# Attention with a fused output projection on one core: units ordered by group of heads, output sums loaded and stored per set

## The reference

```python
xn = _layernorm(x)
qkv = xn @ w_qkv                        # 1024 -> 4096 (q) + 1024 (k) + 1024 (v)
scores = einsum('bqhgd,bkhd->bhgqk', q, k) * 128 ** -0.5
bias = -slopes * sqrt(i - j)            # for j <= i, else -inf (causal)
attn = softmax(scores + bias)
out = einsum('bhgqk,bkhd->bqhgd', attn, v).reshape(B, S, 4096)
attention = out @ w_o                   # 4096 -> 1024
# beside it: ffn = xn @ W.T + b + a low-rank term of the rank that a softmax gate picks
return x + attention + ffn
```

## Time and profile before

| | us |
|---|---|
| median of 3 runs | 2558.14 (2558.04 to 2559.82) |
| the profiled execution's own time | 2558.13 |
| its span, first to last instruction | 2556.3 |
| TensorE busy in the span | 2429.0 (95%) |
| VectorE | 1593.5 (62%) |
| ScalarE | 1442.5 (56%) |
| GpSimd | 884.0 (35%) |

### The profile page before, as it was taken

One profiled execution on the slowest core, in us unless ns is written; L12 is line 12 of the kernel. 1 busy time (PEld: TensorE's weight loads), 2 busy tenths in 40 slices (PEclk: granted clock), 3 DMA queues, 4 the chain that ended last, 5 costly groups with the idle time before them and its releaser, 6 DMA issues.

```text
span 2556.3 us, 35119 instructions
## 1 busy us (share of the span) xinstructions
PE 2429.0 (95%) x12128; PEld 2042.3 (80%) x12128; DVE 1593.5 (62%) x2905; ACT 1442.5 (56%) x3131; POOL 884.0 (35%) x1158
## 2 busy tenths in 40 slices
PE   6999999997999999998899999999999999999998
PEld 4787888885778888887788888888888888888886
DVE  6657445565756445654666777667766776667765
ACT  4432133334533133333877777777777777777774
POOL 3211000001231000000464556545654556445654
PEclk8999999998999999999999999999999999999999
DMA  4546354464355435445613231332334231332221
GB/s 148 183 132 222 116 191 159 176 219 176 103 159 202 153 137 198 169 176 189 227 67 116 102 121 68 115 116 100 110 146 182 100 116 67 124 115 101 80 108 69
DMA packets 94704, 355.25 MB, mean 139 GB/s; under 512 B 8874, under 2 KB 9018, under 8 KB 85569
## 3 DMA queue, kind: packets, MB, share of 16 engines
q1 hardware_dynamic: 62480, 233.43, 25.5%
q0 software_dynamic: 32048, 119.60, 13.5%
HBM read 235.02 MB, written 117.97 MB: 138 GB/s over the span
## 4 chain that ended last, share of the span: by engine, by line
PE 79%; DVE 10%; issue 5%; ACT 4%; DMA 1%; POOL 1%; ACTq 0%; DVEq 0%; SPq 0%; POOLq 0%
PE ps L648 25%; PE ps L650 25%; PE ps L649 25%; PE ps L835 4%; DVE wo L1130 3%; DVE acc L1398 1%; ACT probs L1049 1%; DVE probs L1367 1%; DVE pt_lo L1130 1%; ACT wo L895 1%; ACT res_hi L895 1%; DVE stats L1144 1%; ACT rows L924 1%; DVE w_lo L1130 1%; DMA qk_s<-res_hi 0%
## 5 line engine op out<-in xcount | busy, mean ns | idle before, releaser
L895 ACT ACTIVATE w_hi<-raw 128x1024 fp32r<-128x1024 f32 x196 | 207.0, 1059 | 559.3 <-PE ps L650 440.8
L1130 DVE TENSOR_TENSOR w_lo<-raw,w_hi 128x1024 fp32r<-128x1024 f32 x196 | 239.1, 1224 | 358.2 <-ACT w_hi L895 358.1
L1398 DVE TENSOR_TENSOR acc<-ps,acc 128x512 f32<-128x512 f32 x448 | 296.7, 684 | 226.7 <-issue 195.4
L648 PE MATMUL ps<-x_hi,w_hi 128*128 128x512 f32 x1120 | 436.3, 390 | 0.0
L650 PE MATMUL ps<-x_hi,w_lo 128*128 128x512 f32 x1120 | 435.8, 389 | 0.0
L649 PE MATMUL ps<-x_lo,w_hi 128*128 128x512 f32 x1120 | 435.7, 389 | 0.0
L648 PE MATMUL ps<-wo,op_hi 128*128 128x512 f32 x896 | 367.0, 410 | 50.4 <-issue 30.6
L1035 ACT ACTIVATE probs<-probs,neg_max 128x512 f32<-128x512 f32 (+3 forms) x512 | 283.6, 565 | 200.8 <-DVE neg_max L1367 200.8
L650 PE MATMUL ps<-wo,op_lo 128*128 128x512 f32 x896 | 354.8, 396 | 0.0
L649 PE MATMUL ps<-wo,op_hi 128*128 128x512 f32 x896 | 353.1, 394 | 0.0
L1367 DVE CUSTOM_DVE_ANT_0 probs<-ps,bias 128x512 f32<-128x512 f32 (+3 forms) x512 | 220.3, 484 | 95.3 <-PE ps L650 93.3
(11 more groups left out here) (156 smaller groups left out, 4983.9 us busy)
## 6 DMA issues: line engine op xcount, KB each, us to landing
raw<-w_all SPq DMA_DIRECT2D x70, 1024.0 KB, 5.5
q<-qk_s SPq DMA_DIRECT2D x128, 512.0 KB, 3.3
qk_s<-res_hi POOLq DMA_DIRECT2D x40, 1024.0 KB, 4.6
wo_raw<-w_o SPq DMA_DIRECT2D x64, 512.0 KB, 5.5
qk_s<-res_a POOLq DMA_DIRECT2D x20, 1024.0 KB, 9.1
qk_s<-res_b POOLq DMA_DIRECT2D x20, 1024.0 KB, 5.3
k<-qk_s SPq DMA_DIRECT2D x32, 512.0 KB, 5.7
v<-v_s SPq DMA_DIRECT2D x32, 512.0 KB, 8.5
```

What stands on the lines that cost most here:

```text
L648: pe.matmul(to, st_hi, mv_hi, start=start, stop=False, skip_group_check=True)
L895: nc.scalar.activation(to, source, ACT.Copy).then_inc(signal, 1)
L1130: nc.vector.tensor_tensor(to, source, high.bitcast(F32), ALU.subtract).then_inc(signal, 1)
L1398: nc.vector.tensor_tensor(to, fill[f % 2][:, :], to, ALU.add).then_inc(s_acc, 1)
```

## The change

1. `unit(n)`: the group is outermost, then the pair, the batch and the head. A group's weights are now made once for four sets: 8 makings (`GROUPS`), every 16 units. The bias of the next group is made in the last of the four sets.
2. `acc`: for each set the four tiles of its batch are loaded from `acc_s` (`take_in`) and stored back (`put_out`), to `out` in the last group. Both are issued by SyncE in halves of two tiles.
3. `fills(n)`: the output products of a set start one unit later, (n-2) instead of (n-1), and all loops are one unit longer.
4. `shaped(n)`: the operands of a set are made in a unit ahead of their products; GpSimd does 3, 1, 3 and 1 block sums in the four units and ScalarE its high halves in one place, behind the exponentials.
5. The making: block sums of weights in units F-3 (step 4), F-2 (steps 2, 3) and F-1 (step 5), where F is the unit of first use. High halves: steps 0 and 1 at the end of F-2, 3 and 2 at the end of F-1, 4 and 5 ahead of the exponentials of F, 6 at its end. Low halves: steps 0 and 1 between the sums of F-1, 3 at its end, 2 ahead of the inverses of F, 4 between its sums, 5 and 6 at its end.

```diff
--- before.py
+++ after.py
@@ -55,12 +55,21 @@
...
-OUT_SUMS = ((0, 3), (1, 3), (0, 2), (0, 6), (0, 4), (1, 2), (1, 6), (1, 4))
-OUT_SPLITS = ((), (0, 1), (2, 3, 4), (5, 6))
-WO_SUMS_IN = ((4,), (2,), (3, 5), ())
-GROUPS = SETS // 2
+OUT_SUMS = ((0, 3), (0, 2), (0, 6), (0, 4), (1, 3), (1, 2), (1, 6), (1, 4))
+SUM_SHARES = (range(0, 3), range(3, 4), range(4, 7), range(7, 8))
+GROUPS = KV_HEADS
+GROUP_UNITS = SETS // GROUPS * G
+WO_SUMS = (4, 2, 3, 5)
+WO_SUMS_IN = {7: (4,), 8: (2, 3), 9: (5,)}
+WO_ORDER = (0, 1, 3, 2, 4, 5, 6)
+HIGHS_FIRST = {10: (4, 5)}
+HIGHS_LAST = {8: (0, 1), 9: (3, 2), 10: (6,)}
+LOWS_EARLY = {10: (2,)}
+LOWS_MIDDLE = {9: (0, 1), 10: (4,)}
+LOWS_LAST = {9: (3,), 10: (5, 6)}
@@ -289,27 +298,21 @@
         def unit(n):
-            pr, rest_ = n // (2 * HEADS), n % (2 * HEADS)
-            g, b, h = rest_ // (2 * G), rest_ // G % 2, rest_ % G
-            return pr, g, b, h
+            return n // (2 * G) % PAIRS, n // GROUP_UNITS, n // G % 2, n % G
...
-            s, c = (n - 1) // G - 1, (n - 1) % G
+            s, c = (n - 2) // G - 1, (n - 2) % G
...
-            s, c = n // G - 1, n % G
-            if c == 0:
-                return ([], [(s, 0)]) if 0 <= s < SETS else ([], [])
+            s, c = (n - 1) // G - 1, (n - 1) % G
             if not 0 <= s < SETS:
-                return [], []
-            return {1: ([(s, 1), (s, 2), (s, 3)], [(s, 4), (s, 5), (s, 6)]),
-                    2: ([], [(s, i) for i in range(7, 11)]),
-                    3: ([], [(s, i) for i in range(11, 14)])}[c]
+                return s, [], []
+            return s, [OUT_SUMS[i] for i in SUM_SHARES[c]], list(SHARES[c])
@@ -325,29 +328,21 @@
-        def making(n):
-            group, since = (n - 2) // (2 * G), (n - 2) % (2 * G)
-            return (group, since) if n >= 2 and group < GROUPS and since < G else (None, None)
-        def out_splits(n):
-            group, since = making(n)
-            return [] if group is None else [(group, i) for i in OUT_SPLITS[since]]
-        def out_sums_in(n):
-            group, since = making(n)
-            return [] if group is None else [(group, i) for i in WO_SUMS_IN[since]]
-        WO_SUMS = (4, 2, 3, 5)
+        def making(n, table):
+            group, place_ = (n + G) // GROUP_UNITS, (n + G) % GROUP_UNITS
+            return [(group, i) for i in table.get(place_, ())] if group < GROUPS else []
...
+        def made(group, step):
+            return STEPS * group + WO_ORDER.index(step) + 1
...
-            return PARTS * (2 * group - 1) + STEPS + step + 1
+            return PARTS * (SETS // GROUPS * group - 1) + STEPS + step + 1
@@ -412,7 +407,7 @@
...
                 half, pair = i // 2, i % 2
-                head = group % KV_HEADS * G + 2 * pair
+                head = group * G + 2 * pair
@@ -423,37 +418,46 @@
...
                         out_block(0, i)
-                if n in range(3, 7):
-                    sp.wait_ge(s_store_h, stores_h(2, VALUES, 0))
-                    sp.wait_ge(s_store_a, stores_r(2, VALUES, 0))
-                    sp.wait_ge(s_store_b, stores_r(2, VALUES, 0))
-                    for tt in ((0, 2), (1, 3), (4, 6), (5, 7))[n - 3]:
-                        sp.dma_start(acc[:, tt, :], acc_s[bass.ds(tt * P, P), :]).then_inc(s_acc_in[tt], 16)
-                group = n // (2 * G)
-                if n % (2 * G) == G + 3 and group + 1 < GROUPS:
+                group = n // GROUP_UNITS
+                if n % GROUP_UNITS == 2 * G + 2 and group + 1 < GROUPS:
...
-            def store_out(pr, b, t):
-                tt = b * QT + t
-                sp.dma_start(out[bass.ds((pr * TT + tt) * P, P), :], acc[:, tt, :]).then_inc(s_out[tt], 16)
-            def results(n):
-                for b in range(2):
-                    last = SETS // PAIRS - 2 + b
-                    if n == G * (last + 2) + 3:
-                        for t in range(QT):
-                            sp.wait_ge(s_acc, PARTS * last + (STEPS if t % 2 == 0 else PARTS))
-                            store_out(0, b, t)
-                    if n == G * (last + 2) + 4:
-                        for t in range(QT):
-                            tt = b * QT + t
-                            sp.wait_ge(s_out[tt], 16)
-                            sp.dma_start(acc[:, tt, :], acc_s[bass.ds((TT + tt) * P, P), :]).then_inc(s_acc_in[tt], 16)
+            def sums_home(pr, b, t):
+                return bass.ds((pr * TT + b * QT + t) * P, P)
+            def take_in(s, tile):
+                pr, _, b, _ = unit(s * G)
+                for t in (tile, tile + 2):
+                    if s >= 2:
+                        sp.wait_ge(s_out[b * QT + t], 16 * (s // 2))
+                    sp.dma_start(acc[:, b * QT + t, :], acc_s[sums_home(pr, b, t), :]).then_inc(s_acc_in[b * QT + t], 16)
+            def put_out(s, tile):
+                pr, g, b, _ = unit(s * G)
+                sp.wait_ge(s_acc, PARTS * s + STEPS * (tile + 1))
+                for t in (tile, tile + 2):
+                    to = out if g == GROUPS - 1 else acc_s
+                    sp.dma_start(to[sums_home(pr, b, t), :], acc[:, b * QT + t, :]).then_inc(s_out[b * QT + t], 16)
+            def sums_in_and_out(n):
+                if n == 3:
+                    sp.wait_ge(s_store_h, stores_h(2, VALUES, 0))
+                    sp.wait_ge(s_store_a, stores_r(2, VALUES, 0))
+                    sp.wait_ge(s_store_b, stores_r(2, VALUES, 0))
+                if n in range(3, 7):
+                    take_in((n - 3) // 2, (n - 3) % 2)
+                for s in range(SETS):
+                    since = n - G * s - 10
+                    if since in (0, 2):
+                        put_out(s, since // 2)
+                    if since in (1, 3) and s + 2 < SETS:
+                        take_in(s + 2, since // 2)
@@ -475,13 +479,11 @@
...
                 out_weights(n)
-                results(n)
-            for t in range(2 * QT):
-                sp.wait_ge(s_acc, PARTS * (SETS - 2 + t // QT) + (STEPS if t % 2 == 0 else PARTS))
-                store_out(PAIRS - 1, t // QT, t % QT)
+                sums_in_and_out(n)
+            for n in range(UNITS, UNITS + 3 * G):
+                sums_in_and_out(n)
             for tt in range(TT):
-                sp.wait_ge(s_out[tt], 16 * PAIRS)
+                sp.wait_ge(s_out[tt], 16 * SETS // 2)
@@ -610,35 +612,21 @@
...
                 if step == 5:
-                    pool.wait_ge(s_wo_lo, STEPS * group + 2)
+                    pool.wait_ge(s_wo_lo, made(group, 1))
...
-            for n in range(UNITS + G + 1):
-                at_once, later = shaped(n)
-                s, c = n // G - 1, n % G
-                for group, step in out_sums_in(n) if c == 0 else ():
-                    wo_sums(group, step)
-                if c == 0 and at_once + later:
-                    pool.wait_ge(s_at_raw, G * s + 2)
-                    for tile, k in OUT_SUMS[0:2]:
-                        out_sum(s, tile, k)
-                if at_once:
+            for n in range(UNITS + G + 2):
+                s, new_sums, new = shaped(n)
+                if new_sums:
                     pool.wait_ge(s_at_raw, G * (s + 1))
-                    for tile, k in OUT_SUMS[2:4]:
-                        out_sum(s, tile, k)
-                for part in at_once:
-                    out_low(*part)
-                if at_once:
-                    out_sum(s, *OUT_SUMS[4])
-                if c == 2 and later:
-                    for tile, k in OUT_SUMS[5:8]:
-                        out_sum(s, tile, k)
-                for part in later:
-                    out_low(*part)
-                for group, step in out_sums_in(n) if c != 0 else ():
+                for tile, k in new_sums:
+                    out_sum(s, tile, k)
+                for part in new:
+                    out_low(s, part)
+                for group, step in making(n, WO_SUMS_IN):
@@ -852,8 +840,8 @@
...
                 f = PARTS * s + part
-                if s % 2 == 0 and tile == 0:
-                    pe.wait_ge(s_wo_lo, STEPS * (s // 2) + k + 1)
+                if s % (SETS // GROUPS) == 0 and tile == 0:
+                    pe.wait_ge(s_wo_lo, made(s // (SETS // GROUPS), k))
@@ -1055,7 +1043,7 @@
...
                 if k in (0, 1, 5):
-                    act.wait_ge(s_at_raw, G * s + (2 if k == 0 else G))
+                    act.wait_ge(s_at_raw, G * (s + 1))
@@ -1097,12 +1085,12 @@
...
                 leave(number(pr, MATRICES - 1, STEPS - 1))
-            for n in range(UNITS + G + 1):
-                at_once, later = shaped(n)
+            for n in range(UNITS + G + 2):
+                s, _, new = shaped(n)
...
                     outputs(n - 2)
-                for part in at_once:
-                    out_high(*part)
+                for part in making(n, HIGHS_FIRST):
+                    out_split(*part)
@@ -1110,11 +1098,11 @@
...
                         exponential(n, c)
-                for part in later:
```

(27 more changed lines are left out.)

## The result

Five runs of the changed kernel have a median of 2546.35 us (2544.82 to 2546.99), five of the kernel before, beside them, 2559.82 us (2558.04 to 2561.91). The ratio is **0.9946, with an interval of 0.9932 to 0.9961**: 13.5 us faster by the medians where 54.4 were forecast, and outside the forecast range of 2484 to 2521. The span of the profiled execution went from 2556.3 to 2545.1 us, -11.2.

A forecast was written before the change was run, and what follows sets the result against it. TensorE's gaps were taken to bound the kernel: making stalls of 72.3 us falling to 20.3 (-52.0), the end -1.9 and -0.5, the start 0, sum -54.4. Span 2556.3 becomes 2501.9, plus 1.8 gives 2503.7 us; range 2484 to 2521.

The forecast's parts named there:

- What bounds the kernel: Stage from about 1215 us: TensorE sets the pace, only its gaps can be won; each making costs 4.88 us.
- Groups first: Weights made once per group for all four batches: 8 makings for 16, stalls in the stream from 15 to 7.
- The wait for the copied output goes: In F, products two units after a set's last output give its copy a whole unit's cover, ending that wait.
- The new making, walked through: Engine orders followed through F-1, F and F+1: 2.9 us lost per making, ends 0.3 and 4.9; 7 make 20.3 us.
- each restart of TensorE: Within a making: 0.2 us for each of three restarts of a stopped TensorE, 0.6 us of the 2.9.
- GpSimd and VectorE: Mutual blocking at low halves: longer by at most 0.57 us; at 1.78 us each in F, a making costs about 4.6.
- Sums loaded and stored: Four 512 KB tiles out and in per set, some 190 GB/s for 110; costed at nothing, covered by early issue.
- Rival 3: Slower: sums come late at every set's first addition; 3 us of wait each gives 2594 us; chance 0.04.
- The end: Last set: wait for operands covered, -1.9 us; two stores instead of three behind the last sum, -0.5 us.
- The start: First units and first making: one more unit without products against fewer low halves; taken as 0, ends -3.3 and +4.9 us.
- Rival 2: A making costs as now or more, by low halves or two high halves in F: 2517.7 us, 2539 at 8; chance 0.25.
- what would show it: Signs to check: 158.6 us over 16 units, 1.2 to 1.8 us wait before F's attention product, DMA near 190 GB/s.

The follow-up runs named there:

- group_only: Kernel before with only the group order and the loads and stores of sums; products, operands and weights stay where they were: 2521.21 us, ratio 0.9848.
- high5_last: Changed kernel with the high half of step 5 moved from ahead of the exponential of F to the end of F: 2515.17 us, ratio 0.9824.
- no_sum5: Changed kernel with GpSimd's fourth weight sum cut from 1024 columns to 8, so step 5's operand is not the reference's: 2521.36 us, ratio 0.9852.
- sum5_sooner: spread, with GpSimd's fourth weight sum made between the operands' lows and F's first add ahead of low half 2: 2494.26 us, ratio 0.9746.
- kept_busy: Changed kernel with 50 unread identity transposes on TensorE ahead of the third product of every F: 2531.17 us, ratio 0.9888.
- lows_apart: Changed kernel with low halves 0 and 1 moved within F-1, behind the maxima and ahead of the inverses: 2542.18 us, ratio 0.9937.
- no_traffic: Changed kernel without most stores and loads of the sums and the waits on them, so most output sums are missing: 2544.55 us, ratio 0.9942.
- all_moves: low6_next, with the first group's weights also made one by one from unit 1 on: 2486.23 us, ratio 0.9714.
- low6_next: sum5_sooner with low half 6 moved from the end of F to behind the maxima of F+1: 2493.46 us, ratio 0.974.
- spread: Changed kernel with the weights' high and low halves placed by what waits for them, low half 2 ahead of F's first sum: 2509.99 us, ratio 0.9806.

## Why the prediction missed

The sign held, the number did not. By its own steps:

- **What bounds the kernel: right.** TensorE's gaps, 4.88 us per making before, none elsewhere. Where no making is, the stage runs at 100 of 100 us.
- **Groups first: right.** Seven stalls for fifteen, 56 high halves of weights. group_only has this part alone: 38.8 us, where 72.3 - 7 x 5.3 = 35 of stalls is what its own makings give. They cost 5.3 (5.4 over all seven) and not 4.8 each, with a gap of 2.8 us in F for 2.0 and a fall of the clock behind each of the seven.
- **The wait for the copied output goes: right.** No wait of that kind is left. F-1 lost 1.25 us and now loses nothing, F+1 1.01 and now 0.02.
- **The new making, walked through: this step failed.** It forecast 2.9 us per making, and 8.2 were lost. It asked when VectorE is free for the maxima, a sum and the attention product, and never when **low half 2 is due**. TensorE's third product of F needs it 1424.8 - 1413.1 = 11.7 after T of F-1. By the walk's own times it stands behind the last low copy at 14.8 and takes 1.35: 16.15, so a gap of 4.5 us was in the numbers of the text, unseen. The other 1.5 are the times themselves: the fourth sum ended at 12.5 for 11.3 (the two lengthened lows, 3.41 for 1.45, and the sum, 3.79 for 2.83), the low copies at 16.5 for 14.8, the low half took 1.14. 16.46 + 1.14 + 0.04 = 17.64, and 17.64 - 11.68 = 5.96, the gap. high5_last and no_sum5 show that this chain is the cause, sum5_sooner that without its two waits a making costs 1.6 us, within the 0.3 to 4.9 of the text.
- **A term that was missing: the clock.** The walk took 0.2 us for each restart of TensorE. Behind this gap it runs at 1.2 GHz for 4.7 us, 2.0 us per making and 13.8 us in all (kept_busy). The kernel before had the price too: a fall behind four of its fifteen gaps in F, some 1.1 us each, so it could be read there, and the average of 4.82 holds some of it. The making of the earlier trace rows, from which the walk took its times, is one without a fall.
- **GpSimd and VectorE: undersized.** The text took at most 0.57 us per low half, on VectorE alone. The Trainium skill (SBUF — State Buffer, "Who interferes with whom") calls the shared ports an exclusive lock, so either side can lose; the traces agree: a low part of GpSimd goes from 0.73 to 1.7, four pieces of a sum from 2.8 to 3.8, and a low half of VectorE from 1.21 to 1.84. In lows_apart one low half stayed at 1.21 beside sums of GpSimd that were lengthened. What this adds to the gap stays open, since lows_apart moved it and did not remove it; 4.5 of the 5.96 us come out of the walk's own times without it.
- **Sums loaded and stored: right.** 191 GB/s for the "some 190" forecast, loads land in 5.1 us, no engine waits for one, and no_traffic, without most of them, is 1.8 us faster, no more. Rival 3 did not come.
- **The end: right**, 3.3 us better for its work by the timeline against 2.4 forecast, and the 1.67 us behind the last attention product are gone.
- **The start: wrong**, 0 forecast and 6.0 us lost for its work, just outside the text's ends. Its making has the same chain: TensorE waits 2.49 us at 1252.00 for a low copy and 3.65 at 1266.35 for a low half, and runs slow behind both (0.77 and 0.80). The fall behind the first gap is not certain: in kept_busy, whose code is the same up to there, the gap is 2.50, the matmul behind it takes 0.47 and the unit 9.4 us for 12.2, so 2.8 of the 6.0 us are this fall. all_moves spread those halves over the first seven units and takes 68.5 us from the first T to the ninth for the 71.4 of low6_next.

Of the 43.2 us between forecast and span, 52.0 - 15.7 = 36.3 are the makings, 6.0 the start, 1.8 the stage before (code left alone), and -0.9 the end. **Rival 2** was the case that came, by its strong form of 8 us a making (2539), which the range had left out. Its reason was half right: it named the two high halves ahead of the exponential, but priced them by the weakest number, "as now".

The section on what would show it named 158.6 us from T to T over 16 units; 164.11 lie between two gaps. It named 1.2 to 1.8 us ahead of the attention product as the wait in F; the wait stood one output product earlier.

## What to carry to other kernels

When steps are re-ordered by hand, list for each result that the bound engine reads when it is due and when it is made, every one of them; the one that was left off the list was the one that stalled. Look for the second wait on a slow instruction too, one that is there because a buffer is written over. When a change has two halves, run each alone first: here one gained 39 us and the other threw 25 of them away, and moving the same work within ScalarE's, VectorE's and GpSimd's orders made it 64 gained (sum5_sooner, 2494.26 against 2558.28). Read a price at every repetition and not at one: the one making of high5_last that shows no fall of the clock, and the one of the kernel before in the earlier trace rows, each speak for a part of their kernel only.

## What the hardware showed that was not expected

**The clock behind a gap.** In the kernel after TensorE does nothing for 5.96 us in a stream that is otherwise full, and the matmuls behind it run at 1.2 GHz (granted clock 0.50) for 4.7 us, some 2 us lost. The granted clock also falls to 0.50 behind shorter gaps of F: behind all seven of 3.36 us (no_sum5), all seven of 2.72 to 2.79 (group_only), six of seven of 3.08 (high5_last), six of seven of 2.07 to 2.11 (spread) and four of fourteen of 1.97 to 2.02 (the kernel before), though it did not fall behind its one of 2.76. So a gap of one length, in one place of one kernel, is followed by a fall in one unit and not in another. In these rows the length of the gap alone does not tell whether the clock falls; what does was not tried. 50 idle transposes in the gap of 5.96 us kept it at 1.00.

**A first stage that moves.** Its code is the same in all_moves, sum5_sooner and low6_next, yet the first T of the stage behind it came at 1218.00, 1218.34 and 1224.22 us. In the last, TensorE waits 1.45 us for a DMA at 234.23, and from 236 to 245 us it is busy all the time at a granted clock of 0.50 with 22 matmuls; the other two have 1.00 and 41 there. If the fall lasted some 10 us, as these rows suggest, it cost 5 (an estimate), most of the 6. A difference of a few us between two kernels is better read between two T's within the stage than in medians of four runs.
